# A decoder layer on one core: host-transposed context, weights and mask, first rows normalised by VectorE, opening loads in another order

## What is computed

```python
x = x + self_attention(layernorm(x), W_qk, W_v, alibi_slope)      # one head, causal, scores (xn @ W_qk) @ xn.T / 16 + alibi
x = x + cross_attention(layernorm(x), ctx, ctx, mask, wq, wk, wv, wfc)   # 16 heads of 16; q = xn2 @ wq.T, k = ctx @ wk.T, v = ctx @ wv.T
x = x + moe(layernorm(x), w_gate, w_gate_up, w_down)              # 8 experts, top 2 of the softmax of xn3 @ w_gate
# one expert: (silu(x @ w_g) * (x @ w_u)) @ w_down, inner width 1024
```

## Time and profile before

| | |
|---|---|
| profiled execution, its own time | 1169.76 us |
| its span | 1168.0 us |
| PE busy | 1073.2 us (92%) |
| PEld busy | 909.0 us (78%) |
| DVE busy | 655.6 us (56%) |
| ACT busy | 658.0 us (56%) |
| POOL busy | 524.9 us (45%) |

### The profile page before, as it was taken

The page is one execution under the profiler, slowest core; times in us unless marked ns, Lnnn a source line. Parts: engine busy times, 40 slices in busy tenths (PEclk is TensorE's granted clock), DMA queues, the critical chain, the costliest instruction groups (busy, mean ns, idle before and its releaser), DMA issues.

```text
span 1168.0 us, 37008 instructions
## 1 busy us (share of the span) xinstructions
PE 1073.2 (92%) x12828; PEld 909.0 (78%) x12828; DVE 655.6 (56%) x2156; ACT 658.0 (56%) x1446; POOL 524.9 (45%) x565
## 2 busy tenths in 40 slices
PE   5799989898889988877898999999999999999996
PEld 4466666666666766643888999999999999999996
DVE  6667756666677766664455444444444444444442
ACT  7587877777777888755443444443443444343442
POOL 7656667566666666523224232323323232333322
PEclk9999989999999999988999999999999999999998
DMA  7745444444555454128512144249222121228321
GB/s 228 239 158 166 161 143 141 152 137 140 168 172 171 158 162 149 55 79 274 224 41 35 34 142 137 36 124 361 37 35 32 32 35 28 36 36 297 82 35 19
DMA packets 91671, 142.76 MB, mean 122 GB/s; under 512 B 20960, under 2 KB 69536, under 8 KB 88288
## 3 DMA queue, kind: packets, MB, share of 16 engines
q1 hardware_dynamic: 75790, 122.95, 31.7%
q0 software_dynamic: 15808, 19.09, 9.7%
q10 hardware_dynamic: 18, 0.01, 0.0%
HBM read 268.13 MB, written 43.47 MB: 267 GB/s over the span
## 4 chain that ended last, share of the span: by engine, by line
PE 83%; another core or an unknown queue 4%; DVE 4%; ACT 3%; issue 2%; DMA 1%; POOL 1%; SPq 1%; ACTq 0%; DVEq 0%; POOLq 0%
PE front L2174 16%; PE t_ring L2174 16%; PE pv L2192 8%; PE s_ring L2192 8%; PE pv L1948 6%; PE front L1780 5%; PE t_ring L1933 5%; PE s_ring L1915 5%; PE front L1789 3%; PE s_ring L1767 2%; PE tail L1767 2%; PE tail L1789 2%; PE front L1853 1%; PE front L1767 1%
## 5 line engine op out<-in xcount | busy, mean ns | idle before, releaser
L766 POOL DMA_INDIRECT out<-y_sb,place_i x71 | 112.2, 1580 | 322.7 <-DVE y_sb L1676 131.4
L2174 PE MATMUL t_ring<-rows_hi,wgu_sb 128*128 128x128 f16 x2272 | 214.8, 220 | 1.2 <-issue 1.2
L2174 PE MATMUL front<-rows_hi,wgu_sb 128*128 128x128 f16 x2272 | 214.9, 220 | 0.7 <-issue 0.7
L1207 DVE TENSOR_REDUCE nmax<-s_ring 128x2 f32<-128x512 f32 x256 | 170.3, 684 | 79.6 <-PE s_ring L1915 78.3
L2174 PE MATMUL front<-rows_lo,wgu_sb 128*128 128x128 f16 x1136 | 198.7, 220 | 1.0 <-issue 1.0
L2174 PE MATMUL t_ring<-rows_lo,wgu_sb 128*128 128x128 f16 x1136 | 198.6, 220 | 0.5 <-issue 0.5
L2174 PEld LDWEIGHTS front<-rows_hi,wgu_sb 128*128 128x128 f16 x2272 | 181.2, 98 | 4.1 <-issue 2.5
L2174 PEld LDWEIGHTS t_ring<-rows_hi,wgu_sb 128*128 128x128 f16 x2272 | 181.3, 98 | 2.6 <-issue 0.9
L908 ACT ACTIVATE probs_t<-t_ring,mask_bias 128x512 f32<-128x512 f32 x256 | 170.0, 697 | 21.6 <-PE t_ring L1933 9.7
L1070 ACT ACTIVATE silu_g<-t_ring 128x256 f32<-128x256 f32 x142 | 54.6, 385 | 170.4 <-PE t_ring L2174 164.2
L1070 ACT ACTIVATE silu_g<-front 128x256 f32<-128x256 f32 x142 | 54.4, 384 | 169.4 <-PE front L2174 161.3
(11 more groups left out here) (263 smaller groups left out, 2146.0 us busy)
## 6 DMA issues: line engine op xcount, KB each, us to landing
wgu_sb<-gu_split SPq DMA_DIRECT2D x71, 2048.0 KB
wd_sb<-down_split SPq DMA_DIRECT2D x71, 1024.0 KB
w_piece<-in_w_gu SPq DMA_DIRECT2D x32, 512.0 KB, 5.6
gu_split<-w_halves SPq DMA_DIRECT2D x32, 512.0 KB, 3.6
w_piece<-in_w_down SPq DMA_DIRECT2D x16, 512.0 KB, 6.5
down_split<-w_halves SPq DMA_DIRECT2D x16, 512.0 KB, 4.3
x_in<-in_x SPq DMA_DIRECT2D x16, 256.0 KB, 2.7
ctx_in<-in_ctx SPq DMA_DIRECT2D x16, 256.0 KB, 3.0
```

The source lines that it names most:

```text
L766: nc.gpsimd.indirect_dma_start(out=out, out_offset=bass.IndirectOffsetOnAxis(ap=place_i[:, j:j + 1], axis=0), in_=y_sb[:, j], in_offset=No ...
L1207: nc.vector.tensor_reduce(nmax[:, n // HJ, :, n % HJ], s_ring[n % 2][:].rearrange("p (r k) -> p r k", r=2), AX.X, ALU.max, negate=True).th ...
L2174: o = nc.tensor.matmul(gu_ring[f][:, part * SLOT:(part + 1) * SLOT], wgu_sb[j][:, w, at:at + P], r[:, j % 2, c], start=(i == 0), stop=(i = ...
```

## The change

The host passes ctx transposed, four weights transposed (wq and wk also reordered by head) and the mask both ways. On the device the transposes of context, weights and mask are gone; ScalarE copies `ctx_in` and `w_raw` straight from SBUF, VectorE writes `mask_bias`. VectorE normalises the first rows. The loads of the opening are reordered, w_gate gets a semaphore of its own, for which TensorE waits once before everything else. The stacks of k and q are counted by separate semaphores, so that ScalarE waits for those of k before it overwrites `k_hi`, and for those of q before `q_hi`. `first_fronts` and `iteration` are reordered on all engines. The core of the diff:

```diff
 # SyncE, opening
-            load(0, 0)
-            for i, w in enumerate((w_qk, wk, w_v, wq, wv, wfc)):
+            load_x(0, 0)
+            load_weight(WQK, w_qk)
+            load_ctx(0, 0)
+            load_weight(WK, wk)
+            load_weight(WV1, w_v)
+            sp.dma_start(slope_sb[:], slope.rearrange("(a n) -> a n", a=1).to_broadcast([P, 1])
+                         ).then_inc(slope_loaded, 16)
+            load_x(1, 1)
+            load_weight(WQ, wq)
+            load_ctx(1, 1)
+            load_weight(WV2, wv)
             sp.dma_start(mask_u8[:], mask).then_inc(consts_loaded, 16)
...
+            sp.dma_start(mask_t8[:], mask_t_in.rearrange("(t p) b -> p t b", p=P)).then_inc(consts_loaded, 16)
+            sp.dma_start(wg_sb[:], w_gate.rearrange("(c p) n -> p c n", p=P)).then_inc(gate_loaded, 16)
+            load_weight(WFC, wfc)
...
             def iteration(b, p, h, c, t, s, f, n):
-                if c:
-                    store_stream(b - 1)
                 if n:
                     load_pieces(b + 3, h + 1 + p, 1 - p)
...
                     stack_q_lo(b + 2, p)
+                if c:
+                    store_stream(b - 1)
 # GpSimd
-            rsqrt_norm1(0)
-            f_norm1(0, 0)
...
-            pool.wait_ge(fill_step, 3)
-            nc.gpsimd.dma_start(entries.rearrange("(p j) w -> p j w", p=P), fill[:]).then_inc(scattered[1], FILL)
...
             def first_fronts():
+                rsqrt_norm1(0)
+                ctx_rest(0)
                 xn_rest(0)
-                ctx_rest(0)
+                alibi_select()
                 rsqrt_norm1(1)
+                f_norm1(1, 1)
                 split_lo(0, 0)
-                f_norm1(1, 1)
                 split_lo(0, 1)
+                rsqrt_norm2(0)
+                split_lo(0, 2)
+                xn2_rest(0)
+                ctx_rest(1)
                 xn_rest(1)
...
                 f_norm1(2, 0)
+                fill_entries()
 # ScalarE
+            def f_ctxt(n, p, u):
+                act.wait_ge(ctx_loaded[p], 16 * u + 16)
+                if not isinstance(n, int) or n > 0:
+                    act.wait_ge(v2_ps, n)
+                nc.scalar.activation(ctx_t[:], ctx_in[:, p], ACT.Copy, scale=XSCALE)
+                nc.scalar.activation(ctx_h[:, HI], ctx_in[:, p], ACT.Copy, scale=XSCALE).then_inc(ctxt_sb, 1)
...
             def first_fronts():
+                weight_hi(1)
+                f_ctxt(0, 0, 0)
                 f_xnt(0)
-                f_ctxt(0)
-                split_hi(0, 0, 0, 1)
+                weight_hi(2)
+                weight_hi(3)
                 f_q1(0)
                 f_k(0, 1, 0)
+                weight_hi(4)
+                weight_hi(5)
+                f_v1(0)
+                f_probs(0)
+                split_hi(0, 0, 0, 1)
+                f_probs_t(0)
...
                 f_xnt(1)
+                f_xn2t(0)
+                f_ctxt(1, 1, 0)
+                f_k(1, 0, 1)
+                f_q(0, 1, 0)
 # VectorE
             def first_fronts():
+                value_ones()
+                first_norm()
+                weight_rest(0)
+                weight_rest(1)
                 f_stats1(1, 1, 0)
+                alibi_scale()
+                query_zero()
+                weight_rest(2)
+                masks()
+                f_k(0)
...
+                f_k(1)
+                f_q(0)
+                f_stats1(2, 0, 1)
                 f_scores(1)
                 f_row_max(1)
+                h_max(0, 0, 4)
+                f_aggr1(2)
+                h_max(0, 4, 5)
                 f_sums(1)
+                h_max(0, 5, 6)
                 f_attn(1, 1)
+                h_max(0, 6, 7)
...
             iteration:
                 if c:
                     t_recip(b - 1, 0, tail)
                     t_recip(b - 1, 1, s_ring[1])
+                    t_divide(b - 1, 0, tail)
+                    t_divide(b - 1, 1, s_ring[1])
                 if n:
                     f_aggr1(b + 3)
+                    f_var1(b + 3)
+                if s:
+                    h_max(b + 1, 0, 2)
...
-                    if f == 2 and j % 2 == 0 and not first:
+                    last = isinstance(s, int) and s == NSLOT - 1
+                    if f == (1 if last else 2) and j % 2 == 0 and not first:
                         result(s - 1, (j - 1) % STREAMS)
 # TensorE
-            for i in range(1, 6):
-                pe.wait_ge(raw_loaded[i], 16)
-                transpose_tiles(weight_banks[i - 1], w_raw[:, i]).then_inc(w_tps, 1)
...
             iteration:
                     t_half(b - 1, q, 0, tail)
-                if f:
-                    f_ctxt(b + 2, p, h + 1)
-                if c:
                     t_half(b - 1, q, 1, s_ring[1])
                 if f:
                     f_xnt(b + 2)
-                    f_k(b + 2)
+                if c:
+                    t_ont(b - 1)
                 if t:
                     pe.wait_ge(max_stacked[p], 16 * h + 16)
                     h_scores_t(b, p, 0, 0)
-                if c:
-                    t_ont(b - 1)
+                if f:
+                    f_k(b + 2)
+                    f_q1(b + 2)
                 if t:
                     h_scores_t(b, p, 0, 1)
...
+            pe.wait_ge(gate_loaded, 16)
             attention_loop(pe, first_fronts, iteration)
```

More of the change, by code:

```diff
@@ L74, with decoder_layer @@
 GU_CHUNKS = 2 * F * NC // CHUNK
-def decoder_layer(nc, x, ctx, mask, w_qk, w_v, slope, wq, wk, wv, wfc, w_gate, w_gu, w_down, out):
+def decoder_layer(nc, x, ctx_t_in, mask, mask_t_in, w_qk, w_v, slope, wq, wk, wv, wfc, w_gate, w_gu, w_down, out):
     with ExitStack() as stack:
@@ L1022, in first_fronts @@
                 split_hi(1, 0, 1, 1)
+                f_probs(1)
+                split_hi(1, 1, 1, 1)
+                f_probs_t(1)
+                split_hi(1, 2, 1, 1)
                 f_v2(1, 1)
-                split_hi(1, 1, 1, 1)
-                split_hi(1, 2, 1, 1)
                 f_xn2t(1)
-                f_q(1)
                 h_max(0)
+                f_q(1, 0, 1)
             attention_loop(act, first_fronts, iteration)
@@ L1536, in first_fronts @@
+                weight_rest(4)
+                weight_rest(5)
                 f_sums(0)
@@ L1561, in _ @@
             attention_loop(vec, first_fronts, iteration)
-            step = [1]
+            step = [2]
             def then(ins):
@@ L1841, in f_k @@
                 pe.wait_ge(ctxt_sb, n + 1)
+                if isinstance(n, int) and n == 2:
+                    pe.wait_ge(qlo_sb, 1)
+                elif not isinstance(n, int) or n > 2:
+                    pe.wait_ge(qlo_sb, n)
                 project_t(bank_b(n), WK, ctx_h, 0, OF_HI, start=True)
```

330 lines of the change are left out of this document (139 added, 191 removed).

## The result

The changed kernel takes 1183.0 us (median of four runs, 1182.3 to 1185.3), the kernel before 1168.7 beside it: a ratio of 1.0107, 95% interval 1.0067 to 1.0147 (the two medians alone give 1.0123). It is slower, and outside the forecast's range of 1149 to 1180. The profiled execution of the changed kernel took 1182.3, of which the span is 1180.6, against 1168.0 before.

A forecast was written before the change was run, and what follows sets the result against it. The prediction took TensorE, 91% busy, to fill the loop, its idle time mostly a hold from GpSimd's scatters. Opening -0.8, loop -1.5 and end -1.0 made -3.3 on 1169.8: 1166.5, stated as 1166 us, range 1149 to 1180.

The forecast's parts named there:

- Hold: Loop boundaries: a scatter holds back TensorE's signals until 1.1 us after the last one ends, whatever TensorE ran; chance 0.56.
- rival one: Loop boundaries: the transposes' queue makes the hold, so the 31.6 us idle goes; 1142, or 1153 for half; chance 0.26.
- The half takes the context's place: o_n is ready just when the hold ends.: Loop boundaries: o_t's second half is let go as the context was; -0.3 or +0.1 a boundary, -1.5 us in all.
- my rule's 359.7: Loop boundary: signals come 1.1 us after the last scatter, and o_n is ready 1.24 us after the second reciprocal starts.
- TensorE then does o_n, scores, key and query without a gap: Loop, behind the hold: TensorE runs on until xn's low half; -0.3 us at seven boundaries, +0.1 at six.
- Rival two: Loop: o_n heads TensorE's queue, its wait delays key and scores, the clock falls more often; 1183 us, chance 0.13.
- Opening, -0.8, bounds -5 and +3: Before the loop: the reordered chain sends the first row maximum at 56.2 instead of 56.98 us.
- wg_sb and the removed transposes: Opening: wg_sb lands at about 11.7, bounds 10.87 and 12.7; the removed transposes were hidden behind that load.
- SyncE, "0, at worst some tenths": Loop: store_stream moves to an iteration's end, weight loads go about 6 us earlier behind q_lo; nothing waits for them.
- End, -1.0: Last 15 us: result(69) one step earlier on VectorE lets the last scatter start sooner; -1.0 us, bounds 0 and -2.0.
- the sum of -3.3: Whole kernel: opening -0.8, loop -1.5 and end -1.0 on 1169.8, giving 1166.5 us.

The follow-up runs named there:

- n_key_first3: Changed kernel with the high part of the key projection ahead of o_n's transposes on TensorE, run on the holding chip: ratio 1.0156 to the kernel before.
- n_old_loop: Changed kernel with the loop order of the kernel before on all five engines, less the context's transposes, opening new; holding chip; its own ratio is not given.
- n_host_only: Changed kernel with opening and loop orders of the kernel before; host's transposes, separate semaphores and last result stay: -0.4%, then 0.0% against the kernel before.
- n_old_open: Changed kernel with the opening of the kernel before, less the transposes, and the loop new; holding chip: ratio 1.0110 to the kernel before.
- n_open_warm: Changed kernel with 22 transposes of the identity at the head of TensorE's queue, on a free chip: 1128.2 us, ratio 1.0146 to the kernel before.
- b_store_last: Kernel before with only SyncE's store_stream moved to the end of an iteration: ratio 1.0030 to the kernel before.
- after_again: Changed kernel, unedited, run again beside the kernel before on a free chip: 1126.9 us, ratio 1.0133.
- n_fifth_scatter: Changed kernel with a fifth indirect scatter behind the four of each batch, on a free chip: 1133.7 us, one run.

## Why the prediction was wrong, step by step

**Hold.** Right, in this trace, about where it stands and that it does not need the context's transposes. The stretch stays with the context taken from TensorE (36.0 us before o_n), for VectorE it ends 1.1 us after the last scatter at 7 of 12 boundaries and sooner at the others, and rival one (1142 or 1153) is out. That it comes and goes with the chip was not in the trace.

**"The half takes the context's place: o_n is ready just when the hold ends."** Right in time: 359.54 against my rule's 359.7, and nowhere later than 2.4 us after the last scatter's end. Wrong in what it costs. I counted when the first held operation starts, and gave -1.5; the measured loop is +6.9. The step that failed is the term "TensorE then does o_n, scores, key and query without a gap", with its -0.3 and +0.1 a boundary: it asks when o_n starts and puts what stands behind it at nothing. With the context taken from SBUF, key and first scores can run *inside* the idle stretch; the new order puts them behind its end, and I gave that no price. n_pe_old, the changed kernel with TensorE's old order, runs them inside and needs 8.6 us less in 12 turns: 6.4 less idle time and 2.2 less busy time. That the gain comes from these two alone is argued, not shown: n_key_first3 has the key inside and does not get the time back. The clock was the other half: I reckoned low stretches as before (0.96 mean), and they went from 37 to 55 us, worth 2.8 us. And this account holds for a chip with the hold. On the free chips the same change loses 1.3% with no held stretch, most of it in waits before the next batch's scores and in the opening; my forecast had no such waits, and their cause is open.

**Rival two** gave 1183 and the measurement is 1183, but by the wrong terms: +13.9 in loop and clock, -1 for the rest. Measured is +6.9 in the loop, 5.8 of it in the 12 turns (idle time 3.6, clock 2.8, less 0.55 of busy time for all else), and +6.3 in the opening. That the totals agree is luck. Its mechanism, the key projection behind o_n, is not enough by itself: n_key_first3 has it undone and loses 1.6%. Nor does its sign tell it apart: o_n's wait ends 2.2 us after the last scatter in n_pe_old as well. I had given it 0.13.

**Opening, -0.8, bounds -5 and +3.** Measured +6.3, outside. I followed the chain with old durations and took the gain of 3.6 at softmax for granted; TensorE's work on the first probabilities did come earlier (24.31 against 24.77), but 0.5, not 3.6, and the transposed ones left ScalarE at 26.5, where I had 23.9. Not seen: batch 1's variance now waits on VectorE for TensorE's scores, GpSimd stands idle for 5.13 us, the second rows come at 26.2, and batch 0's attention stands behind them in TensorE's queue. The granted clock was low for 14 us instead of 3.6 ahead of 43 us, and TensorE's first 28 operations, from 12.5 to 19.2 us, ran at the half pace as well (eight in 1.92 us, against 1.04 in the earlier trace rows), though the record of the granted clock reads 1.00 there; I had 16 of them and 1.5 us in all. How much of the +6.3 is the new opening and how much one trace, can be told only roughly. Six traces with the old opening send the first maximum at 56.98 to 58.82, 58.2 on the mean; ten with the new one, edited at most elsewhere, at 59.3 to 64.1, 61.9 on the mean: 3.8 us is my estimate from these, and the profiled 63.32 is one of the late ones. In whole times this is hard to see: n_old_loop to n_host_only is 0.4%, but n_old_open is where the changed kernel is. The range that I gave for opening and end alone was wrong by itself: the bounds add up to 1161 to 1171, not 1162 to 1173.

**wg_sb and the removed transposes.** wg_sb landed at 12.4, I had 11.7 and the bound 12.7. That the removed transposes were hidden, agrees with n_open_warm: 22 put back change nothing that its interval can show.

**SyncE, "0, at worst some tenths".** Too small: b_store_last costs 3.3 us on a free chip. I named the queue and what is behind q_lo, and did not ask what the store's wait had been keeping back. Where TensorE is held anyway it is hidden: in the 12 turns of the profiled kernel the group of the next batch's scores (L1929) has an idle time of 0.0.

**End, -1.0.** Measured -0.9.

**The host's part** by itself is what the sum of -3.3 was close to: -4.4 (-7.6 to -1.2) in one group, +0.5 (-2.1 to +2.9) in the other.

## What to carry to other kernels

A stall that every turn pays is also free room: list what runs inside it or could, and give each move out of it a price, even if the stall ends at the same time. Before moving an instruction that waits, ask what its wait was holding back; here a store's wait was what kept 1.5 MB of loads off a small transfer that was due, and moving it cost the kernel before 3.3 us. Know how far one trace is from the next before reading a few us of it: the same opening ended anywhere in 4.8 us. And split a mixed change by engine early, and on the chip whose loss is to be explained: on the holding chip one engine's order moved the ratio from 1.011 to 0.998, while the single moves had mostly been tried on the others.

## What the runs showed of the hardware

The same program on four chips: 1111, 1112 and 1114 us on three, 1163.5 and 1169.2 on the fourth. On that one and in the trace the prediction rests on, four indirect scatters of GpSimd, 1.28 us apart, went with signals of TensorE arriving up to 1.35 us after the end of the last (in the kernel before 1.0 to 1.35 at 12 of 12 boundaries, in the changed one 1.1 to 1.3 at 7 of 12). On the other three the same scatters, of the same durations (medians 0.97 in both), held nothing: in `after_again` the second reciprocal starts 2.4 us before the last scatter's end. That the scatters make the hold was not tested where it occurs, as `n_fifth_scatter` ran on a free chip. The kernel before takes 32.5 us a turn with the hold and 28.6 without, and the granted clock of its turns is 0.95 and 1.00. What makes the chips differ, the traces do not show.
